# Attention steps re-ordered: transposes ahead of scores, evictions ahead of maxima, and the first half's values moved into their own pair

## The reference

```python
q = (x @ Wq).reshape(b, n, HEADS, DIM_HEAD).transpose(0, 2, 1, 3) * scale
kv = x @ Wkv
kv = jnp.concatenate([jnp.broadcast_to(null_kv, (b, 1, DIM_HEAD)), kv], axis=1)
sim = jnp.einsum('bhid,bjd->bhij', q, kv)
causal_mask = jnp.triu(jnp.ones((i, j), dtype=bool), k=j - i + 1)
sim = jnp.where(causal_mask, mask_value, sim)
attn = jax.nn.softmax(sim.astype(jnp.float32), axis=-1)
out = jnp.einsum('bhij,bjd->bhid', attn, kv.astype(jnp.float32))
return out.transpose(0, 2, 1, 3).reshape(b, n, HEADS * DIM_HEAD) @ Wout
```

## Time and profile before

| | |
|---|---|
| median of 3 runs | 1365.16 us (1363.37 to 1368.6) |
| the profiled execution: its time, its span | 1365.37 us, 1363.2 us |
| mean granted TensorE clock of the span | 0.954 |
| PE, DVE, ACT, POOL busy | 89%, 81%, 68%, 22% |
| the attention | from about 395 us to about 968 us of the span |

### The profile page before, as it was taken

How to read it: one execution, slowest core, us unless ns; L and a number is a source line. 1 busy time by engine, 2 the same in 40 slices (tenths; PEclk the granted TensorE clock), 3 DMA queues, 4 the chain that set the end, 5 groups by cost and what they waited for, 6 DMA issues and landing times. The chain is left out here.

```text
span 1363.2 us, 32364 instructions
## 1 busy us (share of the span) xinstructions
PE 1206.9 (89%) x10992; PEld 516.0 (38%) x10992; DVE 1107.1 (81%) x2001; ACT 925.4 (68%) x1943; POOL 295.8 (22%) x521
## 2 busy tenths in 40 slices
PE   4599999999978899999989898888868999999996
PEld 3122222222245545555565555554641222222222
DVE  6899999998887777777745777776568999999997
ACT  3189999998946655566534566665325999998894
POOL 4300000002103333333312333333321000000200
PEclk9689999999988999999999999999966999999998
DMA  4711212452110000000000000000043222235322
GB/s 103 215 46 53 56 51 71 93 91 66 45 35 19 19 19 19 19 19 19 19 18 19 19 19 19 19 17 2 10 131 106 65 56 51 63 78 100 72 55 62
DMA packets 53809, 70.04 MB, mean 51 GB/s; under 512 B 21264, under 2 KB 31440, under 8 KB 53712
## 3 DMA queue, kind: packets, MB, share of 16 engines
q1 hardware_dynamic: 53712, 68.75, 20.7%
HBM read 37.79 MB, written 22.54 MB: 44 GB/s over the span
## 5 line engine op out<-in xcount | busy, mean ns | idle before, releaser
L914 DVE TENSOR_REDUCE neg_max<-ps 128x1 f32<-128x1024 f32 x512 | 591.5, 1215 | 27.4 <-PE ps L1186 25.4
L750 ACT ACTIVATE arena<-ps 128x512 f32<-128x512 f32 x1024 | 545.4, 598 | 87.6 <-PE ps L1201 75.3
L1201 PE MATMUL ps<-arena 50*128 50x512 bf16 x1024 | 325.0, 389 | 15.4 <-ACT arena L750 10.1
L1217 PE MATMUL ps<-arena 128*32 128x256 f32 (+1 forms) x3584 | 318.0, 427 | 8.7 <-ACT arena L750 3.1
L986 DVE TENSOR_REDUCE a_neg_max<-ps 128x1 f32<-128x129 f32 (+7 forms) x256 | 193.3, 755 | 155.5 <-PE ps L1325 153.8
L1186 PE MATMUL ps<-arena 48*128 48x512 bf16 x1024 | 299.7, 399 | 15.0 <-DVE neg_max L914 14.0
L588 POOL TENSOR_SCALAR arena<-arena,a_rsum 128x128 f32<-128x128 f32 (+7 forms) x256 | 191.2, 747 | 396.0 <-DVE a_rsum L992 395.3
L672 ACT ACTIVATE arena<-ps,a_neg_max 128x129 f32<-128x129 f32 (+7 forms) x256 | 189.6, 741 | 57.9 <-DVE a_neg_max L986 52.8
L678 ACT ACTIVATE arena<-ps 128x64 f32<-128x64 f32 (+7 forms) x256 | 104.5, 408 | 179.2 <-PE ps L1339 177.5
L1318 PE MATMUL ps<-arena 64*128 64x321 f32 (+7 forms) x512 | 192.2, 455 | 11.0 <-ACT arena L672 7.8
L1320 PE MATMUL ps<-arena 64*128 64x128 f32 (+6 forms) x512 | 196.0, 464 | 0.0
(11 more groups left out here) (118 smaller groups left out, 876.6 us busy)
## 6 DMA issues: line engine op xcount, KB each, us to landing
arena<-stack_dram SPq DMA_DIRECT2D x128, 192.0 KB, 3.3
stack_dram<-arena SPq DMA_DIRECT2D x48, 256.0 KB, 3.9
o_dram<-arena SPq DMA_DIRECT2D x32, 256.0 KB, 2.1
arena<-arena SPq DMA_DIRECT2D x32, 256.0 KB, 3.4
arena<-o_dram SPq DMA_DIRECT2D x30, 256.0 KB, 4.2
arena<-max_dram SPq DMA_DIRECT2D x256, 1.0 KB
x<-in_L_attn_x SPq DMA_DIRECT2D x2, 512.0 KB, 4.8
max_dram<-max_T SPq DMA_DIRECT2D x64, 8.0 KB, 1.6
```

The source lines that it names most:

```text
L750: nc.scalar.activation(probs[:, t, :], ps[:, EXP_BANK[t], :], ACT.Exp, scale=F_SCALE).then_inc(probs_ready, 1)
L914: nc.vector.tensor_reduce(neg_max[:, g, t:t + 1], ps[:, bank:bank + 2, :].rearrange("p a b -> p (a b)"), AX, ALU.max, negate=True).then_in ...
L1201: ins = nc.tensor.matmul(ps[:, bank, :], stack[rows, g, 1, kt * P:(kt + 1) * P], stack[rows, g, 0, h * HALF:(h + 1) * HALF], start=True, s ...
L1217: ins = nc.tensor.matmul(ps[row:row + 32, PV_BANK, cols], v_unit[:, g, t // 2, :], probs[:, t, cols], start=j == 0 and c0 == 0 and g % 2 == 0,
```

## The change

Three things are re-ordered; no instruction is added or taken away, and no duration changes. On PE a step issues T(t-4) before S(t). On DVE it issues evD(t-4) before max(t). V0 of a pair is issued in steps 14 and 15 of that pair, no longer in steps 0 and 1 of the next one, and its `o_evac` moves from step 2 to step 0 of the next pair; the first pair of each batch row keeps the old place (`own_values`). ACT and POOL keep their order.

```diff
         V0_STEPS = (0, 1)
+        V0_OWN = (14, 15)
...
+        def own_values(pg):
+
+            return pg not in (0, PAIRS)
...
-                            a_maximum(pg, t)
                             if t >= A_LAG:
                                 a_evac(pg, t - A_LAG)
                             elif not (first and k == 0):
                                 a_evac(pg - 1, NS + t - A_LAG)
+                            a_maximum(pg, t)
...
-                            if t - 1 == V0_STEPS[-1] and not (first and k == 0):
+                            if t == 0 and pg > 0 and own_values(pg - 1) or t - 1 == V0_STEPS[-1] and pg > 0 and not own_values(pg - 1):
                                 o_evac(pg - 1, before[1], 0)
...
-                            a_score_tile(pg, b, k, t, no_q)
                             if t >= A_LAG:
                                 a_transposes(pg, t - A_LAG)
                             elif not (first and k == 0):
                                 a_transposes(pg - 1, NS + t - A_LAG)
-                            if t in V0_STEPS and not (first and k == 0):
+                            a_score_tile(pg, b, k, t, no_q)
+                            if t in V0_STEPS and pg > 0 and not own_values(pg - 1):
...
+                            if t in V0_OWN and own_values(pg):
+                                a_values(pg, b, 0, 2 * pg + 2, V0_OWN.index(t))
...
-                for part in range(2):
-                    a_values(pg, B - 1, 0, 2 * pg + 2, part)
```

More of the change, by code:

```diff
@@ L1410, in body @@
                                 a_transposes(pg - 1, NS + t - A_LAG)
-                            if t in V0_STEPS and not (first and k == 0):
+                            a_score_tile(pg, b, k, t, no_q)
+                            if t in V0_STEPS and pg > 0 and not own_values(pg - 1):
                                 if first and t == V0_STEPS[0]:
                                     pe.wait_ge(av_ready, 2)
-                                if switch and k == 1 and t == V0_STEPS[0]:
+                                if switch and t == V0_STEPS[0]:
                                     pe.wait_ge(x_ready, 2 * B + 2 * b)
```

## The result

The changed kernel takes **1385.07 us** (median of 4 runs, 1381.69 to 1385.92), the kernel before on the same chip 1365.82 (4 runs, 1363.37 to 1368.6). The ratio is 1.0128, 95% interval 1.0102 to 1.0154: slower by 1.3%. The forecast was 1390, the range 1368 to 1404.

What follows compares the result with a forecast made beforehand. PE was busiest but idle some 3.5 us a pair, waiting on DVE and max-exp chains. From 1365.4: steady pairs +21, first pairs +1.5, end -1.2, clock +3, giving 1390 us; range 1368 to 1404, its own 1376 to 1396.

Steps and rivals of the forecast that it cites:

- The chain through ACT: Each step: T(t-2) waits for S(t), max(t), exp(t) and evA(t-3), with one step less cover than before.
- Leg A: Start of max(13) to T(13): 8.41 us against 8.40 before; V0 fills the place of the DVE's jam.
- rival 1: ACT chain does not bind, seam's gain kept: 1.64 us idle go in fourteen pairs, 1342 us; chance 0.08.
- Leg B: T(13) to T(15): 3.03 us against 3.21 before, with POOL's norm(15) ending last.
- Leg C: T(15) to max(9), a stretch where PE sets the pace: 13.9 us against 13.34 before.
- Leg D: max(9) to max(13): 8.44 us against 7.29 before, through max, exp and ACT's evictions.
- The pair: Sum of the four legs: 33.8 us against 32.24, 1.5 us longer; 21 us over fourteen pairs.
- The clock: Added idle time makes dips of PE's granted clock likelier: two more dips, 3 us (bounds 0 to 16).
- Rival 3: A dip of the clock in each pair on top of the forecast: 1387 + 16 = 1403 us; chance 0.24.
- The end: V0 no longer between T(11) and T(12), T(13) waiting for POOL anyway: 1.2 us less (0 to 2.3).
- Rival 2: Gains and losses cancel, idle time kept in the legs does not come: 1359 to 1371 us; chance 0.11.

Runs made afterwards that it cites:

- experiment 3: Changed kernel with ACT copying evA(8) and evA(12) out of PSUM twice: 1396.3 us, ratio to the kernel before 1.0232.
- 4: Kernel before with ACT copying evA(8) and evA(12) out of PSUM twice: 1368.0 us, ratio 1.0016.
- experiment 1: Changed kernel with V0 put back into steps 0 and 1 of the next pair, so only the order differs from before: 1363.94 us, ratio 0.9977.
- 10: Kernel before with V1 at steps 4, 8, 10, 11, V0 split over step 15 and the next pair's step 1, plus the new PE and DVE order: 1351.67 us.
- experiment 7: Changed kernel with V0's first part issued twice, the added pass in step 15 as cover: 1385.39 us, ratio 1.0115.
- experiment 5: Changed kernel with only V0's second part moved behind S(0) of the next pair: 1385.92 us, ratio 1.0131.

## Why the prediction was right, and where it was not

- **The chain through ACT is the cause, as the prediction put it.** Waits moved from "issue" and DVE to ACT's eviction, with 1.37 us before T(13) where about 1.5 was named, and 0.25 to 0.84 before T(6) to T(9). Only the DVE's 12.7 us are more than the "hardly any" of the prediction. Experiments 3 and 4 show that the chain binds in the changed kernel and not in the one before; 1 and 10 show that the order alone makes it.
- **Leg A**, max(13) to T(13): 644.98 - 636.63 = 8.35, forecast 8.41, before 8.35 (the prediction has 8.40, as a first transpose of T(13) stands at 638.62, ahead of the row it read). The DVE's jam went, V0's first part came in its place, and T(13) is as late as it was. This was the step that decided against rival 1.
- **Leg B**, T(13) to T(15): 647.97 - 644.98 = 2.99, forecast 3.03. Its size fits, its reason only in part: the low clock stretches it, and no wait for POOL stands before T(15). That wait appears when the clock does not fall (experiment 7, 0.55 us).
- **Leg C**, T(15) to max(9): 662.55 - 647.97 = 14.58, forecast 13.9. Without a fall it is 13.82 (experiment 1, from T(15) at 639.02 less a pair). So the prediction's 13.9 was the leg, and the remaining 0.76 is the clock.
- **Leg D**, max(9) to max(13): 636.63 - 628.42 = 8.21, forecast 8.44, before 7.29.
- **The pair:** without falls 8.35 + 2.99 + 13.82 + 8.21 = 33.37, and the one clean pair of experiment 5 lasts 33.3; forecast 33.8. The term was 1.56 a pair and should have been 1.1, chiefly by leg D.
- **The clock** is the term that was wrong in kind. Two more dips of 1.61 us were forecast. In fact every pair inside a batch row has one, at about 0.76, and they replace the four of before: over the eleven pairs 11 x 0.76 - 4 x 1.61 = 1.9 us, where 3 was forecast for the whole kernel. Rival 3 thus had the count right and the price wrong, as it took the price of a dip from the earlier trace rows. Its 1403 is out because one fall here costs half of one before. What a fall meets makes the difference. Before, it lay on V0's first part, which took 3.25 us in place of 1.72:

```profile
502.85 3.25 PE L1355 MATMUL ps<-arena 128*64 128x512 f32 x8
```

  In the changed kernel V0 stands ahead of the gap, and the fall meets T(14), T(15) and what follows.
- **The end** was wrong in sign: 1.2 us less was forecast, and 2.5 us more passed from exp(11) of the last pair to the end. exp(11), max(15) and evD(12) there, first before, then after, and T(13) after:

```profile
945.25 1.12 ACT L672 ACTIVATE arena<-ps,a_neg_max 128x1025 f32<-128x1025 f32 x1 [0.56 <-DVE a_neg_max L986]
...
951.94 1.22 DVE L986 TENSOR_REDUCE a_neg_max<-ps 128x1 f32<-128x1025 f32 x1
...
955.73 0.48 DVE L1001 COPY arena<-ps 128x320 f32<-128x320 f32 x1
```

```profile
963.33 1.12 ACT L677 ACTIVATE arena<-ps,a_neg_max 128x1025 f32<-128x1025 f32 x1 [1.23 <-DVE a_neg_max L991]
...
971.82 1.23 DVE L991 TENSOR_REDUCE a_neg_max<-ps 128x1 f32<-128x1025 f32 x1 [0.36 <-PE ps L1330]
...
975.20 0.48 DVE L1006 COPY arena<-ps 128x320 f32<-128x320 f32 x1
```

```profile
975.78 0.59 PE L1344 MATMUL ps<-ident,arena 64*128 64x64 f32 x12 [2.75 <-DVE arena L1006]
```

  In both kernels T(13) starts 0.1 us after evD(12) ends, and evD(12) stands behind the last `recip` and `o_evac` there. So before, neither V0 nor POOL held T(13): its norm(13) had ended at 954.94, 1.37 us ahead of it, and the prediction took the "POOL" of the earlier trace rows at its word. Moving V0 therefore won only 0.41 us between max(15) and T(13) (3.96 against 4.37), while max(15) comes 1.80 later behind exp(11) (8.49 against 6.69), as in the steady pairs (8.50 against 6.69), with V0's first part now ahead of S(15). The other 1.1 us pass behind T(13), where the clock is at 0.50 while T(15) runs (1.00 before).
- **The sum came out closer than its terms.** The profiled execution took 20.6 us more than before, and 24.3 were forecast. The steady pairs were put about 0.4 us too long each, and the end 3.7 us too short; that these two meet is luck.
- **Rival 1** (gain kept, 1342): the seam's gain exists, since V0's move alone gives 1353, but the order takes it back. **Rival 2** (cancel): it is what the new order alone does (1364), not the two together. The prediction didn't see this: it laid the loss on the order (leg D) and took V0 as cover that moves; the runs show that the half with the order costs little as long as V0 covers T(13).

**What stays open:** what decides whether the clock falls. The kernel before, with gaps of at most 0.78 us, fell in four of its eleven pairs, experiment 1, with gaps of up to 1.17, in none, and experiment 3, with 1.84, in some. Also, no run moves ACT's order along with the others, so that this would keep the gain at the seam without the chain is argued only.

## What to carry to other kernels

Where an evacuation is shared out over two engines, look at all of them when a step of the pipeline is moved: here PE and DVE moved one step and ACT kept "exponential, then eviction", which put a maximum, an exponential and a copy between one matmul and the next. Work that can stand anywhere, as V0 and V1, is well put where the engine waits, as between the matmul that starts the longest such chain and the one that ends it; placing it so won 2.5% in the old order. Whether an engine is on the path is tested cheaply by doubling a short instruction on it, and is best read in the legs: 0.47 us in each of two legs of the one kernel, nothing in the other, while the total also carried the clock.

## What the runs showed of the hardware

In the changed kernel, an idle time of 1.37 us on PE, followed by one of 0.31, had the granted clock at 0.57 for the next 4 us in every pair inside a batch row. With 1.65 us of matmul put into that gap it stayed at 1.00, and the time was the same, as the added work cost about what the clock gave back. But a gap of 1.84 us, in experiment 3, left it at 1.00 in five pairs, so the length of one gap does not tell whether a fall comes. The price of a fall goes by the work that it meets: about 0.76 us a pair here, 1.61 in the kernel before, where V0's first part took 1.53 us longer in it.
